# A perceiver block's fp8 layer: where the loop over tiles begins, on four engines

## The chip, the cores and the metric

The kernel runs on one core of a Trainium2 chip. The metric is device time in microseconds (us) for one launch; lower is better. The time before is the median of three runs, 4422.85 us (4418.86 to 4425.76).

## The reference, cut to what matters

The program is a chain of eleven layers on a residual stream of 1024 rows of 256 numbers. The change touches one of them, the cross attention of the fourth block, whose projections work on values rounded to fp8:

```python
def _L3_xattn_ref(hidden_states, cond, ...):
    ln_out = _ln(hidden_states, ln_w, ln_b)
    q = _ln(_fp8_linear_pertensor(ln_out, wq, wq_scale, q_in_scale).reshape(b, s, g, hpg, d), qln_w, qln_b)
    k = _ln(_fp8_linear_pertensor(ln_out, wk, wk_scale, k_in_scale).reshape(b, s, g, d), kln_w, kln_b)
    v = _fp8_linear_pertensor(ln_out, wv, wv_scale, v_in_scale).reshape(b, s, g, d)
    core = _gqa(q, k, v).reshape(b, s, nh * d)
    qx = _ln(_fp8_linear_pertensor(ln_out, wqx, wqx_scale, qx_in_scale).reshape(b, s, g, hpg, d), qxln_w, qxln_b)
    kx, vx = jnp.split(jnp.einsum('bsi,oi->bso', cond, w_kv_x), 2, axis=-1)
    kx = _ln(kx.reshape(b, sc, g, d), kxln_w, kxln_b)
    xout = _gqa(qx, kx, vx.reshape(b, sc, g, d)).reshape(b, s, nh * d)
    catq = _div_clamp_fp8(jnp.concatenate([core, xout], axis=-1), proj_smooth)
    return jnp.einsum('bsi,oi->bso', catq, wproj) * (proj_in_scale * proj_w_scale)
x = x + _L3_xattn_ref(_layernorm(x, axis=-1), ctx_2048, ...)
```

There are 16 query heads and 8 key heads of width 128, 64 own rows per sequence and 128 context rows.

## The kernel before

The layer (`l3_xattn`, from L3365) works through the stream in 8 tiles of 128 rows, two sequences each. Each engine has its own program, a loop over tiles 0 to 6 and a copy of the body for tile 7 behind it; a short stretch ahead of the loop does what the first tile needs. The order inside each program is written out by hand, and the engines meet at semaphores only. All the work of a tile is cut into phases, and phases of tile t+1 are mixed into tile t.

The phases and their names:

- **A head phase** (`HeadPhase`, L683) projects eight heads and normalises each. `fill` (PE, 4 matmuls of 512 columns into two banks, 8 in the trace, where an f32 matmul has two records), `stats_of` (DVE, 8 BN_STATS and 6 small instructions), `invert` (POOL), `normalise` (ACT, writes the rows), `turn` (PE, 8 transposes back into the same banks), `take` (ACT, copies them out and sets `ready`). Both `turn` halves wait for the rows, and whoever fills the pair of banks next first waits for `ready` (`free`, L3427). `x0` and `x1` are the context queries ("x" rows in the trace), `kc0` and `kc1` the context keys, `sk`, `sq0`, `sq1` the own keys and queries of the next tile. `vc0`, `vc1`, `sv` are values without a norm. x0, kc0, vc0, sk and sq1 share one pair of banks; x1, kc1, vc1, sq0 and sv the other.
- **Attention** (`WideAttention`, L784): `score` (PE), `shift` (DVE, subtracts the row maximum), `exponential` (ACT), `weigh` (DVE), `turn` (PE, 8 transposes), `take_turned` (ACT), `mix` (PE), `take_out` (DVE). `own` is the self attention, `cross` the one on the context, in two groups.
- **The norms of the next tile** (`Norm`, L188): `norm` and `ln` on DVE and POOL give `ln_y` (L213), `ln.tensor` (PE, L241, two transposes) and `ln.scalar` (ACT, L255) turn it, `round_inputs` (DVE, L3631) rounds it to fp8 as `xq`, from which every fill but those of the context reads.
- **The output projection** in four quarters (`part_of_y`, L3430: y0 to y3, 8 matmuls of 256 columns, 16 in the trace): y0 and y1 read the self attention, y2 and y3 the cross attention, each once `round_heads` (DVE) has rounded its half. `add_out` (DVE, L3651) adds the bank to the stream, once after y1 and once after y3. The norms of the next tile do not depend on this tile's sum; the stream tile they read is the next one.

In the loop body before, PE's order is: x0.fill, own.score, x1.fill, x0.turn, ln.tensor(t+1), kc0.fill, own.turn 0, x1.turn, own.mix 0, kc1.fill, own.turn 1, kc0.turn, own.mix 1, vc0.fill, kc1.turn, y0, vc1.fill, cross.score 0, sk.fill(t+1), cross.score 1, y1, sq0.fill, cross.turn 0 and on to sq1.turn, y2, y3. DVE's body begins with x0.stats_of, the first half of norm(t+1), own.shift, the second half, own.weigh, ln_y; it ends with round_heads, round_heads, add_out.

```python
                free(sq1, t)
                x0.fill(pe, t)
                pe.wait_ge(cross.out_taken.sem, cross.out_taken.value(t, 0))
                own.score(pe, t, 0)

                free(sv, t)
                x1.fill(pe, t)
                x0.turn(pe, t)
```

Of the kernel before, what the change touches and what calls it, by code (L numbers as in the profile page):

```python
# [82 lines left out]
def whole(program):  # L83

    for _ in program:
        pass
# [3278 lines left out]
def l3_xattn(nc, env):  # L3365
# [3 lines left out]
    with Layer(nc, env, "l3x") as L:  # L3369
# [15 lines left out]
        y_bank, ln_bank = t_bank[0][:, 0:D], t_bank[1]  # L3385
# [40 lines left out]
        def _(pe):  # L3426
# [4 lines left out]
            def part_of_y(t, n):  # L3431
                pe.wait_ge(cat_ready.sem, cat_ready.value(t, n + 1))
                return project(nc, y_bank, lambda c: cat[:, 8 * (n % 2) + c, :], lambda c: wproj[:, 8 * n + c, :], 8, start=n % 2 == 0, stop=n % 2 == 1)
# [14 lines left out]
            def tile(t, more):  # L3448
# [4 lines left out]

                free(sv, t)
                x1.fill(pe, t)
                x0.turn(pe, t)
                if more:
                    whole(ln.tensor(pe, t + 1, ln_bank))

# [3 lines left out]
                if more:  # L3463
                    pe.wait_ge(ln.ready.sem, ln.ready.value(t + 1))
                pe.wait_ge(tile_done.sem, tile_done.value(t, 0))
                own.turn(pe, t, 0)
                x1.turn(pe, t)
                own.mix(pe, t, 0)

                free(x1, t)  # L3470
                kc1.fill(pe, t)
                own.turn(pe, t, 1)
                kc0.turn(pe, t)
                own.mix(pe, t, 1)

                free(kc0, t)
                vc0.fill(pe, t)
                kc1.turn(pe, t)
                part_of_y(t, 0)
# [4 lines left out]
                cross.score(pe, t, 0)  # L3484

# [28 lines left out]
                part_of_y(t, 2)  # L3514
                part_of_y(t, 3).then_inc(y_ps.sem, 1)
# [5 lines left out]
        def _(act):  # L3521
# [7 lines left out]
            def tile(t, more):  # L3529
                o = Order(act, L.order["act"], t)  # L3530
                own.exponential(o, 0)

                x0.normalise(o)
                x0.take(o)
# [4 lines left out]

                x1.normalise(o)  # L3540
                own.take_turned(o, 0)
                x1.take(o)
# [40 lines left out]
        def _(pool):  # L3583
# [5 lines left out]
            def tile(t, more):  # L3589
                o = Order(pool, L.order["pool"], t)  # L3590
                x0.invert(o)
                if more:
                    o.t = t + 1
                    whole(norm.pool(o))
                    whole(ln.pool(o))
                    o.t = t
                x1.invert(o)
# [14 lines left out]
        def _(dve):  # L3612
# [45 lines left out]
            for phase in (sk, sq0, sq1):  # L3658
                phase.stats_of(first)
            def tile(t, more):  # L3660
                o = Order(dve, L.order["dve"], t)
                x0.stats_of(o)
# [5 lines left out]
                own.shift(o, 0)  # L3668
# [11 lines left out]
                x1.stats_of(o)  # L3680
# [4 lines left out]

                kc0.stats_of(o)
                own.take_out(o, 0)

                kc1.stats_of(o)
# [30 lines left out]
                round_heads(o, 1)  # L3720
                dve.wait_ge(y_ps.sem, y_ps.value(t))
# [819 lines left out]
```

## Time and profile before

| | us |
|---|---|
| median of 3 runs | 4422.85 |
| lowest, highest | 4418.86, 4425.76 |
| the profiled execution, its own time | 4422.6 |
| its span | 4420.8 |
| PE busy in the span | 3591.5 (81%) |
| DVE busy | 2633.6 (60%) |
| ACT busy | 1722.9 (39%) |
| POOL busy | 361.6 (8%) |
| mean granted TensorE clock | 0.792 |

The span is the stretch from the first to the last instruction of one profiled execution; 1.8 us lie around it. The shares are means over eleven layers. The layer in question runs from about 2920 us to 3742 us. The granted clock is 1.00 where TensorE has 2.4 GHz and 0.50 where it has 1.2 GHz.

### The profile page before, as it was taken

To read this page: it belongs to the slowest core of one execution; us is meant where nothing else is said; L and a number is where in the kernel's file an instruction comes from. 1 tells how busy PE (TensorE), PEld (TensorE's weight loads), DVE (VectorE), ACT (ScalarE), POOL (GpSimd) and SP (SyncE) were. 2 spreads that over 40 slices of the span, in tenths; PEclk is the share of its full clock that TensorE was granted. 3 is DMA by queue.
4 is the path that set the end of the run, shared out by engine and by line. 5 is a ranking of instruction groups with operands and counts; after the bars stand their busy time and mean duration, and the time that the engine had idled before them with its cause. 6 is when DMAs were issued, how large, how long until landed. Compare 5 with 4: busy or idle time off the path is not lost. (4 is left out here: it accounts for less than half of the span.)

```text
span 4420.8 us, 69997 instructions
## 1 busy us (share of the span) xinstructions
PE 3591.5 (81%) x26672; PEld 2566.4 (58%) x26672; DVE 2633.6 (60%) x5418; ACT 1722.9 (39%) x3305; POOL 361.6 (8%) x566
## 2 busy tenths in 40 slices
PE   7999998997787887753888776878888886878778
PEld 4655557876764555531555643535555555757667
DVE  6888885443367777876444363247667665453552
ACT  4888883111344343421333212224444442223323
POOL 3000000000000000000111000111111111121000
PEclk8555558998886666756988788989999997989787
DMA  2000001000010000010000014000000001200000
GB/s 78 1 0 0 0 0 72 0 0 19 7 36 20 0 0 0 0 58 2 5 5 5 5 59 134 0 3 3 3 5 3 3 3 35 82 0 0 1 1 10
DMA packets 44826, 72.66 MB, mean 16 GB/s; under 512 B 25805, under 2 KB 33489, under 8 KB 41045
## 3 DMA queue, kind: packets, MB, share of 16 engines
q1 hardware_dynamic: 36440, 70.54, 4.6%
q10 hardware_dynamic: 8256, 0.52, 0.2%
q8 instruction: 65, 1.06, 0.1%
q14 instruction: 65, 0.53, 0.0%
HBM read 67.91 MB, written 3.15 MB: 16 GB/s over the span
## 5 line engine op out<-in xcount | busy, mean ns | idle before, releaser
L1316 DVE TENSOR_SCALAR_CACHE_REDUCE l0x_ex<-l0x_s_ps 128x1024 f32<-128x1024 f32 x258 | 305.6, 1222 | 63.4 <-PE l0x_s_ps L1019 62.4
L1151 ACT ACTIVATE l0x_ex<-l0x_ex,l0x_neg_max,l0x_q_scale 128x2048 f32<-128x2048 f32 x128 | 267.9, 2093 | 52.4 <-DVE l0x_neg_max L1322 50.7
L1031 PEld LDWEIGHTS l0x_t_ps<-l0x_identb,l0x_pb 128*128 128x128 bf16 x2048 | 200.0, 142 | 109.4 <-issue 56.8
L1019 PE MATMUL l0x_s_ps<-l0x_kT,l0x_qT 64*128 64x512 bf16 x516 | 235.5, 600 | 32.9 <-ACT l0x_qT L1146 19.5
L1158 ACT ACTIVATE l0x_pt<-l0x_t_ps 128x1024 bf16<-128x1024 bf16 x256 | 246.3, 1014 | 32.2 <-PE l0x_t_ps L1031 32.2
L1031 PE MATMUL l0x_t_ps<-l0x_identb,l0x_pb 128*128 128x128 bf16 x2048 | 233.7, 304 | 6.8 <-ACT l0x_pt L1158 4.1
L1331 DVE TENSOR_SCALAR l0x_pb<-l0x_ex 128x2048 bf16<-128x2048 f32 x128 | 156.4, 1222 | 0.0
L263 PE MATMUL l3x_bank<-l3x_wproj,l3x_cat 128*128 128x256 f32 x512 | 120.7, 390 | 32.1 <-DVE l3x_cat L3345 32.1
L263 PE MATMUL l3x_bank<-l3x_w_kv_x,l3x_ctxT 128*128 128x512 f32 x256 | 129.8, 655 | 0.9 <-ACT l3x_ctx_q L762 0.9
L263 PEld LDWEIGHTS l3x_bank<-l3x_wproj,l3x_cat 128*128 128x128 f32 x512 | 96.1, 193 | 52.4 <-DVE l3x_cat L3345 38.7
L1019 PEld LDWEIGHTS l0x_s_ps<-l0x_kT,l0x_qT 64*128 64x128 bf16 x516 | 50.0, 121 | 129.4 <-issue 80.4
L840 ACT ACTIVATE l3x_e<-l3x_e 128x1024 f32<-128x1024 f32 x24 | 25.4, 1057 | 251.0 <-DVE l3x_e L860 251.0
L885 DVE TENSOR_TENSOR l2x_oT<-l2x_bank,l2x_bv 128x512 f32<-128x512 f32 x32 | 20.6, 686 | 168.6 <-PE l2x_bank L834 168.6
L834 PE MATMUL l2x_bank<-l2x_pt,l2x_v 128*128 128x64 f32 x512 | 95.9, 374 | 29.9 <-ACT l2x_pt L845 29.9
L707 PE MATMUL l3x_bank<-ident,l3x_rows 128*128 128x128 f32 x448 | 69.3, 294 | 61.1 <-ACT l3x_rows L755 61.1
L834 PEld LDWEIGHTS l2x_bank<-l2x_pt,l2x_v 128*128 128x128 f32 x512 | 93.1, 285 | 38.2 <-issue 32.0
L2112 PEld LDWEIGHTS l1a_bank<-l1a_u,l1a_gm 64*64 64x64 f32 x2048 | 109.4, 218 | 8.8 <-issue 7.9
L2112 PE MATMUL l1a_bank<-l1a_u,l1a_gm 64*64 64x8 f32 x2048 | 112.4, 249 | 0.0
L2252 ACT ACTIVATE l1a_decay<-l1a_bank 128x512 f32<-128x512 f32 x64 | 34.7, 594 | 190.9 <-PE l1a_bank L2093 190.9
L2093 PE MATMUL l1a_bank<-l1a_steps,l1a_after 128*128 128x512 f32 x132 | 105.3, 891 | 0.0
L707 PEld LDWEIGHTS l3x_bank<-ident,l3x_rows 128*128 128x128 f32 x448 | 53.4, 149 | 85.9 <-ACT l3x_rows L755 78.5
L2092 PE MATMUL l1a_bank<-l1a_same,l1a_later 64*128 64x512 bf16 x66 | 32.7, 495 | 82.4 <-DVE l1a_steps L2358 82.4
(740 smaller groups left out, 8651.6 us busy)
## 6 DMA issues: line engine op xcount, KB each, us to landing
l3x_wproj<-in_L_xattn_wproj SPq DMA_DIRECT2D x1, 4096.0 KB, 22.5
l3a_w<-in_L_attn_W SPq DMA_DIRECT2D x4, 1024.0 KB, 11.4
l2f_w<-in_L_ffn_w SPq DMA_DIRECT2D x1, 2816.0 KB, 12.4
l0x_ctxT<-in_ctxT SPq DMA_DIRECT2D x8, 256.0 KB, 3.0
l0a_wq<-in_L_attn_W_Q SPq DMA_DIRECT2D x1, 2048.0 KB
l0a_wk<-in_L_attn_W_K SPq DMA_DIRECT2D x1, 2048.0 KB
l0a_wv<-in_L_attn_W_V SPq DMA_DIRECT2D x1, 2048.0 KB, 8.0
l0a_wo<-in_L_attn_W_O SPq DMA_DIRECT2D x1, 2048.0 KB, 13.0
```

The lines of the kernel that those rows point to most:

```text
L263: ins = nc.tensor.matmul(out, wT(c), rhs(c), start=start and n == 0, stop=stop and n == chunks - 1)
L707: ins = self.L.nc.tensor.transpose(self.banks[u][:, h * P:(h + 1) * P], self.rows[:, 4 * u + h, :], self.L.env.ident[:])
L834: ins = self.L.nc.tensor.matmul(out[:, b * S:(b + 1) * S], self.v(half * 8 + h, b), self.pt[:, h, b * S:(b + 1) * S], start=True, stop=True)
L1019: ins = mm(s_ps[:, j * 512:(j + 1) * 512], qT[rows, h // 2, :], kT[rows, h // 2, j * 512:(j + 1) * 512], start=True, stop=True)
L1031: ins = nc.tensor.transpose(t_ps[:, j * P:(j + 1) * P], pb[:, h % 2, j * P:(j + 1) * P], identb[:])
L1151: s.activation(ex[:, h % 4, :], ex[:, h % 4, :], ACT.Exp, scale=q_scale[:, h:h + 1], bias=nb[:, h:h + 1], accum_out=sums[:, h:h + 1]).then ...
L1158: s.activation(pt[:, h % 2, c], t_ps[:, c], ACT.Copy).then_inc(o.up(pT_taken), 1)
L1316: v.tensor_scalar(ex[:, h % 4, c], s_ps[:, c], 1.0, None, ALU.mult, ALU.max, accum_out=mx[:, h, half:half + 1]).then_inc(o.up(scores_taken ...
L1331: v.tensor_scalar(pb[:, h % 2, :], ex[:, h % 4, :], MAGIC, -MAGIC, ALU.add, ALU.add).then_inc(o.up(probs), 1)
L2093: ins = mm(bank[4 + j][:], after[:], flat(steps_[:, 8 * j:8 * j + 8, :]), start=False, stop=True)
L2112: ins = mm(bank[6][r, h * HP:(h + 1) * HP], gm[r, h, :], u[r, h * HP:(h + 1) * HP], start=True, stop=True)
L2252: s.activation(flat(decay[:, h:h + 8, :]), bank[4 + j][:], ACT.Exp).then_inc(o.up(exp_ready if j else None), 1)
```

## The change

PE: x0.fill, own.score, x1.fill become a function `begin`, called once ahead of the loop for tile 0, and in the body for tile t+1 between y2 and y3. The body begins with x0.turn. ln.tensor(t+1) goes behind kc0.fill, x1.turn ahead of own.turn 0, kc1.fill ahead of own.mix 0, vc0.fill ahead of own.mix 1, vc1.fill directly behind kc1.turn, and y0 behind cross.score 0. ACT: the body begins with the rows of x0, the exponential comes behind x0.take, the rows of x1 ahead of ln.scalar. POOL: x1.invert goes between the two norms. DVE: x0.stats_of and own.shift of tile t+1 go to the end of tile t, ahead of the second add_out; the body begins with the first norm's statistics, then x1.stats_of; kc0.stats_of goes ahead of round_inputs, kc1.stats_of ahead of own.take_out 0.

```diff
@@ -3445,43 +3445,45 @@
             free(sq0, 0)
             sv.fill(pe, 0)
             sq1.turn(pe, 0)
-            def tile(t, more):
+
+            def begin(t):
                 free(sq1, t)
                 x0.fill(pe, t)
                 pe.wait_ge(cross.out_taken.sem, cross.out_taken.value(t, 0))
                 own.score(pe, t, 0)
-
                 free(sv, t)
                 x1.fill(pe, t)
+
+            begin(0)
+            def tile(t, more):
                 x0.turn(pe, t)
-                if more:
-                    whole(ln.tensor(pe, t + 1, ln_bank))
-
                 free(x0, t)
                 pe.wait_ge(ctx_loaded.sem, ctx_loaded.value(t))
                 kc0.fill(pe, t)
                 if more:
+                    whole(ln.tensor(pe, t + 1, ln_bank))
+                x1.turn(pe, t)
+                if more:
                     pe.wait_ge(ln.ready.sem, ln.ready.value(t + 1))
                 pe.wait_ge(tile_done.sem, tile_done.value(t, 0))
                 own.turn(pe, t, 0)
-                x1.turn(pe, t)
-                own.mix(pe, t, 0)
 
                 free(x1, t)
                 kc1.fill(pe, t)
+                own.mix(pe, t, 0)
                 own.turn(pe, t, 1)
                 kc0.turn(pe, t)
-                own.mix(pe, t, 1)
 
                 free(kc0, t)
                 vc0.fill(pe, t)
+                own.mix(pe, t, 1)
                 kc1.turn(pe, t)
-                part_of_y(t, 0)
 
                 free(kc1, t)
                 vc1.fill(pe, t)
                 pe.wait_ge(own.out_taken.sem, own.out_taken.value(t))
                 cross.score(pe, t, 0)
+                part_of_y(t, 0)
 
                 free(vc0, t)
                 if more:
@@ -3512,6 +3514,8 @@
                     sv.fill(pe, t + 1)
                     sq1.turn(pe, t + 1)
                 part_of_y(t, 2)
+                if more:
+                    begin(t + 1)
                 part_of_y(t, 3).then_inc(y_ps.sem, 1)
             with pe.Fori(0, TILES - 1) as t:
                 tile(t, True)
@@ -3528,18 +3532,17 @@
             sv.take(first)
             def tile(t, more):
                 o = Order(act, L.order["act"], t)
-                own.exponential(o, 0)
-
                 x0.normalise(o)
                 x0.take(o)
+                own.exponential(o, 0)
+
+                x1.normalise(o)
                 if more:
                     o.t = t + 1
                     whole(ln.scalar(o, ln_bank, scale=ln_w, bias=ln_b))
                     o.t = t
-
-                x1.normalise(o)
+                x1.take(o)
                 own.take_turned(o, 0)
-                x1.take(o)
 
                 kc0.normalise(o)
                 own.take_turned(o, 1)
@@ -3592,9 +3595,12 @@
                 if more:
                     o.t = t + 1
                     whole(norm.pool(o))
+                    o.t = t
+                x1.invert(o)
+                if more:
+                    o.t = t + 1
                     whole(ln.pool(o))
                     o.t = t
-                x1.invert(o)
                 kc0.invert(o)
                 kc1.invert(o)
                 if more:
@@ -3657,15 +3663,16 @@
             round_inputs(first)
             for phase in (sk, sq0, sq1):
                 phase.stats_of(first)
+            x0.stats_of(first)
+            own.shift(first, 0)
             def tile(t, more):
                 o = Order(dve, L.order["dve"], t)
-                x0.stats_of(o)
                 if more:
                     o.t = t + 1
                     first_norm, second_norm = norm.vector(o, tile_of(env.x, t + 1)), ln.vector(o, norm.y[:])
                     next(first_norm)
                     o.t = t
-                own.shift(o, 0)
+                x1.stats_of(o)
                 if more:
                     o.t = t + 1
                     whole(first_norm)
@@ -3677,16 +3684,13 @@
                     whole(second_norm)
                     o.t = t
 
-                x1.stats_of(o)
+                kc0.stats_of(o)
                 if more:
                     o.t = t + 1
                     round_inputs(o)
                     o.t = t
-
-                kc0.stats_of(o)
+                kc1.stats_of(o)
                 own.take_out(o, 0)
-
-                kc1.stats_of(o)
                 own.take_out(o, 1)
                 dve.wait_ge(own.out_taken.sem, own.out_taken.value(t, 1))
                 round_heads(o, 0)
@@ -3718,6 +3722,11 @@
                 round_heads(o, 0)
                 dve.wait_ge(cross.out_taken.sem, cross.out_taken.value(t, 2))
                 round_heads(o, 1)
+                if more:
+                    o.t = t + 1
+                    x0.stats_of(o)
+                    own.shift(o, 0)
+                    o.t = t
                 dve.wait_ge(y_ps.sem, y_ps.value(t))
                 add_out(o, tile_done)
                 dve.wait_ge(o.sem, o.at())
```

No instruction is added or taken away per tile. The two places below are those on which the steps of the next section rest. PE around the branch that closes the loop (COMPARE_AND_BRANCH); wqx is the weight of x0 and x1, own_k the own score, rows a turn, w_kv_x a context fill, pb the turn of the own probabilities, wproj a quarter of y. Before:

```order
L263 MATMUL l3x_bank<-l3x_wproj,l3x_cat 128x256 x8
L3432 REGISTER_ALU
L263 MATMUL l3x_bank<-l3x_wproj,l3x_cat 128x256 x8
L3516 REGISTER_ALU
L3516 COMPARE_AND_BRANCH
```

Now:

```order
L263 MATMUL l3x_bank<-l3x_wproj,l3x_cat 128x256 x8
L263 MATMUL l3x_bank<-l3x_wqx,l3x_xq 128x512 x4
L814 MATMUL l3x_bank<-l3x_own_k,l3x_own_q 64x64 x32
L263 MATMUL l3x_bank<-l3x_wqx,l3x_xq 128x512 x4
L3432 REGISTER_ALU
L263 MATMUL l3x_bank<-l3x_wproj,l3x_cat 128x256 x8
L3520 REGISTER_ALU
L3520 COMPARE_AND_BRANCH
```

The two fills and the score of the next tile went from behind the branch to between y2 and y3. DVE where its loop starts (the ISA row is the loop's own register work), now; ahead of it now stand, once, the 14 instructions of x0.stats_of and the 4 of own.shift that the body before began with:

```order
L860 TENSOR_TENSOR l3x_e<-l3x_bank,l3x_self_mx 128x512
L858 TENSOR_REDUCE l3x_self_mx<-l3x_bank 128x8
L860 TENSOR_TENSOR l3x_e<-l3x_bank,l3x_self_mx 128x512
L3734 UNCONDITIONAL_BRANCH
L3734 ISA
L206 BN_STATS l3x_n_stats<-x_stream 128x6
L207 ISA
L209 BN_AGGR l3x_n_mv<-l3x_n_stats 128x2
L210 REGISTER_ALU
L713 ISA
L715 BN_STATS l3x_x_stats<-l3x_bank 128x6 x4
```

The loop's first instruction is now the statistics of the stream, and it lies 18 instructions further on in DVE's program.

## Rows read from the trace of the kernel before

**Rows 1.** DVE's timeline (start, length, engine, line, what, [idle before]): `add_out`.

```profile
3061.61 0.48 DVE L3651 SCALAR_TENSOR_TENSOR x_stream<-l3x_bank,l3x_out_scale,x_stream 128x256 f32 x1 [3.89 <-PE l3x_bank L263]
...
3645.10 0.48 DVE L3651 SCALAR_TENSOR_TENSOR x_stream<-l3x_bank,l3x_out_scale,x_stream 128x256 f32 x1 [3.89 <-PE l3x_bank L263]
```

**Rows 2.** PE's timeline over one turn of the loop, 3150 to 3256 us.

```profile
3150.16 2.21 PE L263 MATMUL l3x_bank<-l3x_wproj,l3x_cat 128*128 128x256 f32 x9 [1.33 <-DVE l3x_cat L3345]
...
3161.84 2.08 PE L814 MATMUL l3x_bank<-l3x_own_k,l3x_own_q 128*64 128x64 f32 x64
...
3173.25 1.12 PE L707 MATMUL l3x_bank<-ident,l3x_rows 128*128 128x128 f32 x4 [5.70 <-ACT l3x_rows L755]
...
3176.42 0.69 PE L241 MATMUL l3x_bank<-ident,l3x_ln_y 128*128 128x128 f32 x2 [0.66 <-DVE l3x_ln_y L213]
3176.90 4.94 PE L263 MATMUL l3x_bank<-l3x_w_kv_x,l3x_ctxT 128*128 128x512 f32 x8
...
3212.44 3.70 PE L263 MATMUL l3x_bank<-l3x_wk,l3x_xq 128*128 128x512 f32 x8
...
3252.25 3.72 PE L263 MATMUL l3x_bank<-l3x_wproj,l3x_cat 128*128 128x256 f32 x16 [0.88 <-DVE l3x_cat L3345]
```

**Rows 3.** DVE's timeline behind the branch back, the same turn.

```profile
3158.59 0.48 DVE L3651 SCALAR_TENSOR_TENSOR x_stream<-l3x_bank,l3x_out_scale,x_stream 128x256 f32 x1 [3.89 <-PE l3x_bank L263]
3162.50 0.30 DVE L715 BATCH_NORM_STATS2 l3x_x_stats<-l3x_bank 128x6 f32<-128x128 f32 x1 [3.42 <-PE l3x_bank L263]
3164.74 1.48 DVE L715 BATCH_NORM_STATS2 l3x_x_stats<-l3x_bank 128x6 f32<-128x128 f32 x7 [1.95 <-issue]
...
3167.97 0.69 DVE L858 TENSOR_REDUCE l3x_self_mx<-l3x_bank 128x8 f32<-128x512 f32 x1
...
3170.63 0.40 DVE L213 TENSOR_SCALAR l3x_n_y<-x_stream,l3x_n_mv,l3x_n_rstd 128x256 f32 x1
...
3175.95 0.41 DVE L213 TENSOR_SCALAR l3x_ln_y<-l3x_n_y,l3x_ln_mv,l3x_ln_rstd 128x256 f32<-128x256 f32 x1
```

**Rows 4.** DMA queues (packets, MB, share): instruction queue in 3159.4:3161.5 and 3161.5:3164.

```profile
q14 instruction: 1, 0.01, 0.9%
...
q14 instruction: 1, 0.01, 1.2%
```

**Rows 5.** DVE's timeline where the loop is left for the last tile.

```profile
3646.73 0.89 DVE L715 BATCH_NORM_STATS2 l3x_x_stats<-l3x_bank 128x6 f32<-128x128 f32 x4 [1.15 <-PE l3x_bank L263]
```

**Rows 6.** POOL's and ACT's timeline: x0's scale, then its rows.

```profile
3169.34 0.20 POOL L746 TENSOR_TENSOR l3x_x_nmean<-l3x_x_mean,l3x_x_rstd 128x8 f32<-128x8 f32 x1
...
3171.71 2.89 ACT L755 ACTIVATE l3x_rows<-l3x_bank,l3x_x_nmean,l3x_x_rstd 128x128 f32<-128x128 f32 x8
```

**Rows 7.** PE's and ACT's timeline: own.turn 1, kc0.turn, kc0.take; kc1.turn, kc1.take.

```profile
3193.50 1.04 PE L821 MATMUL l3x_bank<-ident,l3x_pb 128*128 128x128 f32 x8
...
3195.55 1.45 ACT L762 ACTIVATE l3x_ctx_k<-l3x_bank,l3x_kxln_b,l3x_kxln_w 128x512 f32<-128x512 f32 x2
...
3201.04 1.04 PE L707 MATMUL l3x_bank<-ident,l3x_rows 128*128 128x128 f32 x8
...
3201.68 1.45 ACT L762 ACTIVATE l3x_ctx_k<-l3x_bank,l3x_kxln_b,l3x_kxln_w 128x512 f32<-128x512 f32 x2 [1.16 <-PE l3x_bank L707]
```

**Rows 8.** Windows (length, busy PE, PEld, DVE, ACT, POOL, granted clock, DMA); PE's timeline.

```profile
3172.40:3179.50 7.10, 5.32 (x14) 2.97 (x15) 6.79 (x22) 4.45 (x11) 0.63 (x2) 0.53 0.00 0
...
2951.82 6.62 PE L263 MATMUL l3x_bank<-l3x_wq,l3x_xq 128*128 128x512 f32 x8 [0.87 <-ACT l3x_own_k L762]
```

**Rows 9.** First tile: `ln_y` on DVE and the next tile's sk.fill on PE.

```profile
2981.56 0.41 DVE L213 TENSOR_SCALAR l3x_ln_y<-l3x_n_y,l3x_ln_mv,l3x_ln_rstd 128x256 f32<-128x256 f32 x1
...
3017.96 3.70 PE L263 MATMUL l3x_bank<-l3x_wk,l3x_xq 128*128 128x512 f32 x8
```

**Rows 10.** Last tile, PE: y2 of the tile before, and cross.score 1.

```profile
3636.66 3.72 PE L263 MATMUL l3x_bank<-l3x_wproj,l3x_cat 128*128 128x256 f32 x16 [1.33 <-DVE l3x_cat L3345]
...
3694.67 3.40 PE L814 MATMUL l3x_bank<-l3x_ctx_k,l3x_ctx_q 128*64 128x128 f32 x32 [3.00 <-DVE l3x_e L860]
```

## The prediction

> **What bounds the kernel now.** I read the timelines of PE and DVE over one turn of the loop of the fp8 layer. One turn is one `add_out` to the next: six turns take 3645.10 - 3061.61 = 583.5 us, 97.25 each [rows 1]. PE is the engine the others follow: between two y2 it works almost without a break, save one place. x1.fill ends at 3167.55, and x0.turn starts 5.70 us later, when ACT has written the first rows of x0 [rows 2]. The reader is to see why the rows are late: x0.fill was over by 3161.9, since own.score starts at 3161.84 [rows 2], but DVE, which takes the statistics, ended `add_out` at 3159.07, did one BN_STATS at 3162.50 and the other seven only from 3164.74 [rows 3]. The 3.43 us up to the first are the branch back, since where the loop is left without one, the first statistics come 1.15 us after `add_out` [rows 5]. The 1.95 us after the first wait for nothing ("issue"), and the instruction queue fetches a block in each of the two gaps [rows 4]. So 5.4 us of DVE's restart lie on the path x0.fill, rows, x0.turn, and behind it the layer norm of the next tile, whose ln.tensor waits again.
>
> **What the change does to that path.** I count from the start of y2 to the start of the next sk.fill; behind it nothing changes order up to the next y2. Before, that is 3212.44 - 3150.16 = 62.3 us [rows 2], in a turn of 97.5 us (`add_out` at 3158.59 [rows 3], y3's end 0.1 before the next one at 3252.25 + 3.72 [rows 2]); the mean turn is 0.25 shorter, so I take 62.0. Now, with y2 at 0:
>
> 1. y2 3.6, x0.fill 3.5, own.score 2.0, x1.fill 3.6, y3 3.7 (a fill as sk.fill 3.70 less the overlap of 0.15 with what follows, the rest as [rows 2] has it) without a wait: y3's rounding came 0.88 us too late behind y2, now 9 us of work cover it. y3 ends at 16.4.
> 2. x0.turn does not wait. x0.fill ends at 7.1, statistics 2.2 us after it at 9.3, scale at 11.4, the eight rows take 2.9 us [rows 6]: ready at 14.3, 1.9 us before PE asks. DVE's own.shift fits between. The stall of 5.70 us is gone.
> 3. kc0.fill needs x0.take, which needs x0.turn, and ln.tensor no longer stands between. From the start of kc1.turn to the end of kc1.take are 2.1 us, 1.1 beyond the turn [rows 7]. So kc0.fill runs from 18.4 to 22.0.
> 4. **What is late next is ln_y.** The second `add_out` now follows y3 at 16.4 instead of 7.3 + 0.9, ends at 16.95 (0.12 + 0.48), and only behind it DVE branches. Then 3.43 for the branch, 3.4 for x1.stats_of and the stream's statistics (3164.74 to 3167.97, and 0.2 for the one instruction ahead of the gap), 5.3 from n_y to the end of own.weigh, 0.4 for ln_y [rows 3]: 29.5. PE waits for it from 22.0: **7.6 us, the one large stall that is left.** Behind ln.tensor are queued x1.turn, own.turn, kc1.fill and all the rest of the tile.
> 5. The gap of 1.95 I take as gone. It lies directly behind the loop's first instruction, where a fetch happens; the loop's head now lies 18 instructions further on. Behind the second fetch DVE runs on to the end of ln_y, 11 us and some 40 instructions, without such a gap [rows 3], so edges lie much further apart than 18 instructions, and one that is met after some microseconds of work costs nothing. Lowest price of the gap in the changed kernel: none; highest: the full 1.95.
> 6. From 29.6: ln.tensor 0.5; x1.turn and own.turn at the low clock 2.2 and 2.1 (x0.turn's halves took 1.12 each, against 1.04 for a whole turn at the high one [rows 2, 7]); kc1.fill 4.9 as kc0.fill had it behind today's stall [rows 2]; own.mix 0 1.9: 41.1. own.turn 1, kc0.turn and kc0.take 3.6 [rows 7], of which 1.65 are a new wait, since own.mix no longer covers the take; vc0.fill 3.4; own.mix 1 1.9; kc1.turn and its take 2.15, with 1.1 of wait, also new; vc1.fill 3.5; cross.score 1.9; y0 3.6: sk.fill at 61.2. y0's own wait goes, because the rounding ends 2 us before it.
>
> So 62.0 becomes 61.2: the stall of 5.70, the gap of 1.95, the waits around x1.turn and the low clock over own.mix 0 go, and a wait of 7.6 and three of 1.1 to 1.65 come. **0.8 us a turn, 5 us for six.**
>
> The first and last tile are extra. At the first, DVE walks into the loop without a branch back: ln_y starts at 2981.56 plus 2.6 for x1.stats_of (as step 4 counts it, 3.4 less 0.8 for the stream) plus 0.4 because the exponential now stands behind x0.take, 2984.6 [rows 9]. From there the count of step 6 with turns and fill at the high clock, and about 1 us of small waits, is 29 us: sk.fill at 3014 instead of 3017.96, and up to 3016 if the clock falls, as it did under the fill at 2951.82. I take 3.3 us (2 to 4.3). At the last tile there is no norm and no branch. Before, y2 to cross.score 1 is 3694.67 - 3636.66 = 58.0 us [rows 10]. Now x1's rows are ready at 24.6 and the chain of step 6 without ln_y gives own.mix 1 at 38.7, then take_out 1.3, two roundings of 4.4 and own shift 2.7: cross.score 1 at 53.6. That is 4.4 less, and 1.4 more if the score then runs at the high clock. I take 4.8 (2.5 to 5.7).
>
> Sum: 5 + 3.3 + 4.8 = 13.1 us off the profiled execution's 4422.6, which stands 0.25 below the median: **4409.5 us**.
>
> **A rule against step 5.** The trace shows 1.95 us of DVE standing still with a fetch in it. The Trainium skill (Runtime: NRT & Kernel Launch, Instruction fetch mechanics) says that a taken branch out of the current two-page window forces a fetch before execution goes on, but of crossing a block's edge in sequence that it is "one DMA tail-bump, mostly hidden". By the first half the 3.43 us stay, which the trace bears out; by the second there would be no gap of 1.95 us to lose, and the sum would be that of the second rival below, 4421; here the trace speaks against it, since the gap stands behind the same instruction in every turn of this loop.
>
> **What is uncertain.** The clock after the new stall. The granted clock was 0.53 from 3172.4 to 3179.5, that is the lower level for nearly all of it, after PE had stood from 3167.55 [rows 8, 2]. Step 6 has own.mix 0 at the high clock, since no wait stands ahead of it any more. Lowest price: both turns and the fill at the high clock, 3.6 us less than taken, 22 us over six turns, if PE were back at once; the rows after the present stall speak against it, but a part of it can come. Highest: kc1.fill all at the low clock, 6.6 as at 2951.82 [rows 8], 1.7 us a turn more, 10 us over six. I take the value of the same stall today, since length and work behind it are nearest.
>
> **Rivals.**
> - *The forecast* (0.57): 4409.5, its own range 4402 to 4414.
> - *The clock comes back sooner* behind the stall (0.13): 1 to 3.6 us a turn less, 4388 to 4403.
> - *The gap of 1.95 us moves along with the loop's head*, because a restart always costs two fetches (0.12): ln_y 1.95 later in six turns, 11.7 us, 4421, no change. For it: it is in every turn. Against: it comes after one instruction, which looks like an edge.
> - *The clock stays low through kc1.fill* (0.12): 10 us more, 4419, no change.
> - *Slower*: the moved norm chain (0.06). ln_y now starts 8 us later relative to PE's work, and any further delay of it goes one to one into the turn, where today x0.turn and x1.turn absorb a part. Should DVE's restart meet two more gaps of 1.95, in x1.stats_of and in own.weigh, the turn grows by 3.9, six by 23.4: 4433. It decides from 3.7 us a turn upward (13.1 + 8.9 over six). For it: two gaps stand there today. Against: behind the second fetch none of today's instructions waits.
> - That x0.turn still waits has a margin of 1.9 us and would cost only what exceeds it.
>
> **Numbers.** About 0.2% (8.8 us) is what a measurement of this kernel can tell from no change: below 4414.0 is faster, above 4431.7 slower. The forecast is faster save its upper edge, the second case always, the third and fourth are in the same band, the fifth slower. Faster 0.67, same 0.27, slower 0.06. The range leaves out the ends of the sooner clock and the slower case: 4397 to 4421.
>
> **What would show it.** In the changed profile: x0.turn starts right behind y3; DVE's first statistics 3.4 us after `add_out`, and no idle "issue" of 1.95 behind it; PE waits 7 to 8 us for ln_y at L241, in front of it kc0.fill with a wait of about 1.1; waits of 1.6 and 1.1 at vc0.fill and vc1.fill on ACT; one stretch at the low clock per turn; a turn of 96.4 us. A wait at L241 of 9 us or more says that the gap is still there; kc1.fill above 6 us says that the clock is. I am wrong altogether if x0.turn still waits, or if a long wait stands at a fill or at cross.turn where I have none.

## The result, and the profile after

The changed kernel takes 4382.8 us (median of 4 runs, 4379.7 to 4386.3) against 4423.5 us for the kernel before (4 runs): a ratio of 0.9907, 95% interval 0.9891 to 0.9922. It is faster by 41 us. The forecast was 4409.5: the direction was right, the size was not, and the time lies outside the range of 4397 to 4421.

The span of the profiled execution fell from 4420.8 to 4377.9 us. Part of that is no effect: the layers ahead of this one took 8.4 us less, with the same instructions. So I measure the layer by itself, from VectorE's (DVE's) first statistics in it to its last `add_out`, in the timeline of DVE. Before:

```profile
2923.65 0.43 DVE L206 BATCH_NORM_STATS2 l3x_n_stats<-x_stream 128x6 f32<-128x256 f32 x1
...
3741.47 0.48 DVE L3651 SCALAR_TENSOR_TENSOR x_stream<-l3x_bank,l3x_out_scale,x_stream 128x256 f32<-128x256 f32 x1 [4.63 <-PE l3x_bank L263]
```

After:

```profile
2915.24 0.43 DVE L206 BATCH_NORM_STATS2 l3x_n_stats<-x_stream 128x6 f32<-128x256 f32 x1
...
3694.42 0.48 DVE L3657 SCALAR_TENSOR_TENSOR x_stream<-l3x_bank,l3x_out_scale,x_stream 128x256 f32<-128x256 f32 x1 [5.29 <-PE l3x_bank L263]
```

That is 817.8 us before and 779.2 after, 38.6 less. This measure repeats: another execution of the changed kernel gives 779.6, while its whole span is 10 us longer than the first; 9.1 us of that lie ahead of this layer. PE over one turn of the changed loop, to compare with [rows 2]:

```profile
3131.99 3.72 PE L263 MATMUL l3x_bank<-l3x_wproj,l3x_cat 128*128 128x256 f32 x16 [1.33 <-DVE l3x_cat L3345]
...
3144.63 3.62 PE L263 MATMUL l3x_bank<-l3x_wproj,l3x_cat 128*128 128x256 f32 x16
3148.08 1.04 PE L707 MATMUL l3x_bank<-ident,l3x_rows 128*128 128x128 f32 x8
3150.30 3.70 PE L263 MATMUL l3x_bank<-l3x_w_kv_x,l3x_ctxT 128*128 128x512 f32 x8 [1.18 <-ACT l3x_ctx_q L762]
3158.72 0.69 PE L241 MATMUL l3x_bank<-ident,l3x_ln_y 128*128 128x128 f32 x2 [4.72 <-DVE l3x_ln_y L213]
3159.20 1.91 PE L707 MATMUL l3x_bank<-ident,l3x_rows 128*128 128x128 f32 x8
3160.91 1.91 PE L821 MATMUL l3x_bank<-ident,l3x_pb 128*128 128x128 f32 x8
3162.61 4.26 PE L263 MATMUL l3x_bank<-l3x_w_kv_x,l3x_ctxT 128*128 128x512 f32 x8
3166.72 1.95 PE L831 MATMUL l3x_bank<-l3x_pt,l3x_own_v 128*128 128x128 f32 x16
3168.50 1.04 PE L821 MATMUL l3x_bank<-ident,l3x_pb 128*128 128x128 f32 x8
...
3172.05 3.70 PE L263 MATMUL l3x_bank<-l3x_w_kv_x,l3x_ctxT 128*128 128x512 f32 x8 [1.64 <-ACT l3x_ctx_k L762]
...
3179.51 3.70 PE L263 MATMUL l3x_bank<-l3x_w_kv_x,l3x_ctxT 128*128 128x512 f32 x8 [1.10 <-ACT l3x_ctx_k L762]
...
3188.59 3.60 PE L263 MATMUL l3x_bank<-l3x_wk,l3x_xq 128*128 128x512 f32 x8
```

The order is as forecast, with the small waits of 1.18, 1.64 and 1.10, x0.turn (3148.08) without a wait, and one large wait for `ln_y` at L241. But this wait is 4.72 us, not 7.6. DVE's timeline says why; compare [rows 3]:

```profile
3148.29 0.48 DVE L3657 SCALAR_TENSOR_TENSOR x_stream<-l3x_bank,l3x_out_scale,x_stream 128x256 f32 x1 [4.34 <-PE l3x_bank L263]
3149.44 0.43 DVE L206 BATCH_NORM_STATS2 l3x_n_stats<-x_stream 128x6 f32 x1 [0.67 <-DVEq L3733]
3150.02 0.18 DVE L209 BATCH_NORM_AGGREGATE l3x_n_mv<-l3x_n_stats 128x2 f32<-128x6 f32 x1 [0.15 <-DVEq L208]
...
3158.25 0.41 DVE L213 TENSOR_SCALAR l3x_ln_y<-l3x_n_y,l3x_ln_mv,l3x_ln_rstd 128x256 f32<-128x256 f32 x1
```

Between `add_out` and the first statistics there are 0.67 us, where 3.4 had been, and the gap of 1.95 is gone too. **The branch itself had become cheap.** The page's row of the queue that brings in DVE's instructions, before and then after:

```profile
q14 instruction: 65, 0.53, 0.0%
```

```profile
q14 instruction: 35, 0.29, 0.0%
```

30 packets fewer, which is five for each of six turns. In the turn from 3150 to 3247 us of the kernel before, this queue has 5 packets of 8192 B; in that from 3149 to 3240 us of the changed one it has none.

### The profile page after: what moved, and what is told of

Its sections match the earlier page's. It is cut to its first block and busy times, and to the rows that moved or that the text cites. A ratio compares the mean times of both kernels' runs of the same rounds, so it can differ in the third digit from the quotient of the medians.

```text
span 4377.9 us, 69990 instructions
## 1 busy us (share of the span) xinstructions
PE 3565.0 (81%) x26672; PEld 2558.8 (58%) x26672; DVE 2633.0 (60%) x5418; ACT 1723.9 (39%) x3305; POOL 359.3 (8%) x566
## 3 DMA queue, kind: packets, MB, share of 16 engines
q8 instruction: 65, 1.06, 0.1%
## 5 line engine op out<-in xcount | busy, mean ns | idle before, releaser
L1019 PE MATMUL l0x_s_ps<-l0x_kT,l0x_qT 64*128 64x512 bf16 x516 | 235.5, 600 | 32.8 <-ACT l0x_qT L1146 19.5
L834 PE MATMUL l2x_bank<-l2x_pt,l2x_v 128*128 128x64 f32 x512 | 91.8, 363 | 28.7 <-ACT l2x_pt L845 28.7
L885 DVE TENSOR_TENSOR l3x_cat<-l3x_bank,l3x_smooth_inv 128x512 f32<-128x512 f32 x64 | 41.2, 685 | 108.4 <-PE l3x_bank L834 68.7
L263 PEld LDWEIGHTS l3x_bank<-l3x_w_kv_x,l3x_ctxT 128*128 128x128 f32 x256 | 50.0, 206 | 87.9 <-issue 60.7
L263 PE MATMUL l2f_bank<-l2f_w,l2f_ln_yT 128*128 128x352 f32 x256 | 97.4, 512 | 0.0
```

Of the source, the lines that this page charges most:

```text
L263: ins = nc.tensor.matmul(out, wT(c), rhs(c), start=start and n == 0, stop=stop and n == chunks - 1)
L834: ins = self.L.nc.tensor.matmul(out[:, b * S:(b + 1) * S], self.v(half * 8 + h, b), self.pt[:, h, b * S:(b + 1) * S], start=True, stop=True)
L885: v.tensor_tensor(self.oT[:, h:h + 4, :], ps, by[:, h:h + 4].unsqueeze(2).broadcast_to([P, 4, P]), op).then_inc(o.up(self.out_taken if j e ...
L1019: ins = mm(s_ps[:, j * 512:(j + 1) * 512], qT[rows, h // 2, :], kT[rows, h // 2, j * 512:(j + 1) * 512], start=True, stop=True)
```

## What could be behind it

The queue brings DVE's program in by blocks. In what follows an edge is the border between two blocks, the head is the first instruction of the loop, the place is where the head lies in its block, and the restart is the time that DVE stands between `add_out` and its first operation behind the branch back.

**Theory A, the place in the blocks.** In the first tile of the kernel before, a packet arrives each time DVE has begun about 128 more instructions (5543, 5672 and 5804 of those recorded). So I take a block of 8192 B to hold 128 instructions, and the counts tell roughly where its edges lie: the old loop (269 instructions, the register and semaphore ones included) began 2 ahead of an edge and touched four blocks; the new one (268) begins 18 later, 16 behind that edge, and touches three. If DVE can hold four blocks and always brings in the next one, a loop over three stays, and a loop over four throws out its own beginning: five packets a turn. (DVE's turn has one semaphore instruction fewer in the trace after, 268 for 269, although the section on the change says that none is taken away.)

**Theory B, the order.** The instructions that now follow the branch, or the work that now overlaps it, hide the restart.

The experiments put idle instructions ahead of the loop (increments of a semaphore that nobody reads, 0.093 us each, where DVE waits 7.33 us for PE in the kernel before and 7.74 in the changed one). They move the loop in the blocks and change nothing in it. In the kernel before with three of them:

```diff
+            pad = L.sem("pad")
             first = Order(dve, L.sem("dve_first_order"))
@@
-            for phase in (sk, sq0, sq1):
+            for phase in (sk, sq0):
                 phase.stats_of(first)
+            for _ in range(3):
+                dve.sem_inc(pad, 1)
+            sq1.stats_of(first)
```

All results (ratio to the kernel before with its interval; the layer as measured above; a turn as a sixth of six; the packets of DVE's instruction queue in the whole program). The kernel before was timed again beside each set of runs: 4423.0 us beside the b runs and a110_old_place, 4419.5 beside a102_edge_ten_on, aln, v0_y3_in_the_middle and v1, 4423.4 beside the others. So two runs of different sets are compared by their ratios, or by the layer.

| run | edit | us | ratio | layer | turn | packets |
|---|---|---|---|---|---|---|
| before | | 4423 | | 817.8 | 97.2 | 65 |
| b1_one_extra | before + 1 | 4418.7 | 0.9997 (0.9983 to 1.0011) | 817.3 | 97.3 | 66 |
| b3_three_extra | before + 3 | 4401.4 | 0.9951 (0.9933 to 0.9968) | 800.1 | 94.0 | 35 |
| b20_twenty_extra | before + 20 | 4403.1 | 0.9955 (0.9937 to 0.9972) | 799.8 | 94.0 | 35 |
| after_again | | 4384.9 | 0.9908 (0.9893 to 0.9922) | 779.6 | 91.7 | 36 |
| a110_old_place | after + 110 | 4412.8 | 0.9987 (0.9976 to 0.9999) | 806.5 | 95.7 | 71 |
| a102_edge_ten_on | after + 102 | 4412.9 | 0.9981 (0.9972 to 0.9990) | 809.6 | 95.9 | 71 |
| a90_far_from_edge | after + 90 | 4387.8 | 0.9923 (0.9911 to 0.9936) | 779.4 | 91.8 | 41 |
| a90_twelve_inside | + 90, 12 inside | 4405.6 | 0.9966 (0.9953 to 0.9980) | 800.5 | 95.5 | 71 |
| aln_norm_turn_early | order, PE | 4414.5 | 0.9982 (0.9973 to 0.9991) | 809.9 | 95.7 | 35 |
| v0_y3_in_the_middle | order, PE | 4351.6 | 0.9847 (0.9831 to 0.9863) | 749.4 | 87.6 | 36 |
| v0_old_place | v0 + 110 | 4389.8 | 0.9927 (0.9914 to 0.9939) | 780.0 | 92.3 | 72 |
| v1_and_norms_first | order, three engines | 4376.6 | 0.9908 (0.9893 to 0.9924) | 772.3 | 90.9 | 35 |

## Experiments on the place

> The kernel before with ONE idle VectorE instruction (an increment of a semaphore that nobody reads) ahead of the l3x loop, in a stretch where VectorE waits over 7 us for TensorE. Theory A (place in the blocks: VectorE's code comes in blocks of 8192 B, 128 instructions; before, the loop of 269 instructions begins 2 ahead of a block's edge and touches four blocks, and the trace shows all of them and one more brought in again each turn; the changed kernel's loop begins 16 behind an edge, touches three, and the trace shows none brought in again): the head now lies 1 ahead of the edge, still four blocks: five fetches a turn, 2.9 to 3.1 us behind the branch, 4423 us within 0.2%. Theory B (the new order of the work, not the place, took the restart away): no change either, 4423 us. This kernel is the control for the next one.

> The kernel before with THREE such instructions ahead of the loop; nothing else differs from the kernel before. Theory A: the head lies 1 behind the edge, the loop touches three blocks: no fetch in the loop, the branch costs 0.3 us in place of 3.06, the gap of 1.95 is gone, the wait of x0.turn falls from 5.70 to about 1; a turn falls from 97.25 to 92.5 to 94.5, the time to 4388 to 4404 us. Theory B: 4423 us within 0.2%, five fetches a turn.

> The kernel before with TWENTY such instructions: the head lies 18 behind the edge, nearly as in the changed kernel (16). Theory A: as with three, within 0.15% of it (4388 to 4404 us). Theory B: 4423 us within 0.2%. What it lacks to the changed kernel's 4383 us is what the new order is worth at an equal place: by theory A at most 20 us, by theory B all 41.

One idle instruction changes nothing; **three make the kernel before 0.49% faster**, with not one instruction of the loop changed, and twenty do the same. Theory B is out as the whole cause. DVE and PE with three:

```profile
3159.12 0.48 DVE L3651 SCALAR_TENSOR_TENSOR x_stream<-l3x_bank,l3x_out_scale,x_stream 128x256 f32 x1 [3.89 <-PE l3x_bank L263]
3160.76 0.89 DVE L715 BATCH_NORM_STATS2 l3x_x_stats<-l3x_bank 128x6 f32<-128x128 f32 x4 [1.15 <-PE l3x_bank L263]
```

```profile
3170.38 0.66 PE L707 MATMUL l3x_bank<-ident,l3x_rows 128*128 128x128 f32 x4 [2.29 <-ACT l3x_rows L755]
```

The statistics come 1.15 us behind `add_out`, as where the loop is left in the kernel before [rows 5]. x0.turn waits 2.29 us where it had waited 5.70 [rows 2]; I had expected about 1. The turn falls by 3.3 us and not by the 4 to 5 that DVE gains, since its statistics now wait for x0.fill itself.

> The CHANGED kernel with 110 such instructions ahead of the loop (some 7 us of VectorE's time in a wait of 7.74 us for TensorE): its head lies 2 ahead of an edge, as in the kernel before. Theory A: four blocks, five fetches a turn, about 3 us behind the branch and 1.95 at the edge, the wait of ln.tensor for l3x_ln_y rises from 4.72 to 8 to 10, a turn from 92.1 to 95.5 to 97.5, the time to 4404 to 4420 us. Besides, the loop of the next layer (l3a, 311 instructions) then touches four blocks too, and its fetches must appear in every turn of it, which adds up to 20 us more. Theory B: 4383 us within 0.2%, no fetch in the loop.

The reverse, and it comes as theory A has it: 71 packets, and both gaps are back, at the new instructions:

```profile
3154.52 0.48 DVE L3657 SCALAR_TENSOR_TENSOR x_stream<-l3x_bank,l3x_out_scale,x_stream 128x256 f32 x1 [4.34 <-PE l3x_bank L263]
3158.39 0.43 DVE L206 BATCH_NORM_STATS2 l3x_n_stats<-x_stream 128x6 f32 x1 [3.39 <-issue]
3160.79 0.18 DVE L209 BATCH_NORM_AGGREGATE l3x_n_mv<-l3x_n_stats 128x2 f32<-128x6 f32 x1 [1.97 <-DVEq L208]
```

The wait at L241 is 9.25 us in place of 4.72. In the layer after this one (l3a), whose loop of 311 instructions now touches four blocks as well, the one branch back costs 3.04 us in place of 0.33. From this layer's last `add_out` to the span's end are 687.4 us, against 683.5 in the changed kernel; but in two other kernels with the same loss in l3a (a90_far_from_edge, v0_old_place) they are 683.4, so this part of the time is not settled by it. The 110 instructions took 10.5 us, not the 7 of the expectation, and the first tile up to sk.fill is 1.9 us longer (92.7 against 90.8).

> The CHANGED kernel with 102 idle VectorE instructions ahead of the loop, in place of the 110 of a110_old_place: its head lies 10 instructions ahead of a block's edge, not 2, so the loop still touches four blocks. Theory A (place in the blocks): five fetches a turn; the branch still costs about 3 us, and the second gap stands 8 instructions further on and is shorter by the time of these, some 1 us in place of 1.97, since the second block is asked for as soon as the first has landed. The wait of ln.tensor is 8.2 to 8.7 us in place of 9.25, a turn 94.5 to 95.5 us in place of 95.7, the time 4400 to 4412 us. Should the gap sit at l3x_n_mv again, it belongs to the operation and not to the edge. Theory B (the gap belongs to what was reordered): as the changed kernel, 4383 us.

```profile
3160.99 0.43 DVE L206 BATCH_NORM_STATS2 l3x_n_stats<-x_stream 128x6 f32 x1 [4.21 <-issue]
3161.57 0.18 DVE L209 BATCH_NORM_AGGREGATE l3x_n_mv<-l3x_n_stats 128x2 f32<-128x6 f32 x1 [0.15 <-DVEq L208]
3161.88 0.69 DVE L715 BATCH_NORM_STATS2 l3x_x_stats<-l3x_bank 128x6 f32<-128x128 f32 x3
3163.47 1.09 DVE L715 BATCH_NORM_STATS2 l3x_x_stats<-l3x_bank 128x6 f32<-128x128 f32 x5 [0.90 <-issue]
```

The second gap left l3x_n_mv and stands in the middle of a group of equal statistics, at 0.90 us: it belongs to the place in the code and to no operation. What I had not expected is that the first gap grew from 3.39 to 4.21, so that nothing was gained: the wait at L241 is 9.26 us, a turn 95.9, both above the expectation. In all six turns two packets start within 0.7 us of each other just behind the branch (here at 3158.00 and 3158.42); in a110_old_place only one starts there (3156.26), and the restart is 3.39. a90_twelve_inside below has such a pair too (3148.60 and 3149.09) and a restart of 4.17. So the pair goes with the longer restart; that the two packets delay each other was not tested by itself.

> The CHANGED kernel with 90 idle VectorE instructions ahead of the loop: its head lies 22 ahead of a block's edge, and its 268 instructions just fit into three blocks (106 + 268 = 374 of 384). Theory A1 (what counts is how many blocks the loop touches; four with the one brought in ahead are too many): no fetch in the loop, 0.3 us behind the branch, a turn of 92.1 us; 4383 us and up to 5 more, since the next layer's loop (l3a) now touches four blocks. Theory A2 (what counts is that the head lies ahead of an edge, a few instructions or some): fetches each turn, 4400 to 4412 us.

> As a90_far_from_edge, and twelve idle VectorE instructions INSIDE the loop as well, ahead of the wait for y_ps, where VectorE waits 4.34 us: they take 12 times 0.093 us, 1.1 us, of that wait. The loop now has 280 instructions and ends 2 behind the last edge: four blocks. Theory A1: five fetches a turn, 3.4 to 4.3 us between add_out and l3x_n_stats, but no second gap (the next edge is 22 instructions on); the wait of ln.tensor 7.3 to 8.3 us in place of 4.72, a turn 94 to 95.5 us, 4398 to 4408 us, which is the case that the prediction on record took the change for. Theory A2, or that only the head counts: within 0.1% of a90_far_from_edge.

```diff
+                for _ in range(12):
+                    dve.sem_inc(pad, 1)
                 dve.wait_ge(y_ps.sem, y_ps.value(t))
                 add_out(o, tile_done)
```

The two have the loop's head at the same place, 22 ahead of an edge, and differ only in where the loop ends. With 268 instructions it fits three blocks and the restart is free; with 280 it ends 2 instructions inside a fourth. It is the number of blocks that counts (A1), not the head's closeness to an edge. In the second kernel, as expected, there is one gap and no second:

```profile
3146.93 0.48 DVE L3657 SCALAR_TENSOR_TENSOR x_stream<-l3x_bank,l3x_out_scale,x_stream 128x256 f32 x1 [4.34 <-PE l3x_bank L263]
3151.58 0.43 DVE L206 BATCH_NORM_STATS2 l3x_n_stats<-x_stream 128x6 f32 x1 [4.17 <-issue]
3152.16 0.18 DVE L209 BATCH_NORM_AGGREGATE l3x_n_mv<-l3x_n_stats 128x2 f32<-128x6 f32 x1
```

Its restart is 4.17 - 0.67 = 3.5 us longer; six of them are 21.0, and the layer is 800.5 - 779.4 = 21.1 us longer. Whatever DVE loses at the branch goes one to one into the turn. PE's wait at L241, all six turns (groups by line, 3058 to 3610 us), in the changed kernel and then in this one:

```profile
L241 PE MATMUL l3x_bank<-ident,l3x_ln_y 128*128 128x128 f32 x12 | 3.9, 422 | 28.4 <-DVE l3x_ln_y L213 28.4
```

```profile
L241 PE MATMUL l3x_bank<-ident,l3x_ln_y 128*128 128x128 f32 x12 | 4.1, 449 | 50.1 <-DVE l3x_ln_y L213 50.1
```

What the four corners give, by the layer: old order 817.8 at the old place and 800.1 at a good one; new order 806.5 at the old place (a110_old_place) and 779.2 at its own. **Of the 38.6 us, 17.7 to 27.3 are the place and 11.3 to 20.9 the order**, by which is changed first. The 27.3 hold 1.9 us of the first tile, which is longer behind the 110 idle instructions; the six turns alone give 19.7 us for the place in the old order and 23.6 in the new. It is worth more in the new order; the likely reason is that there nothing absorbs a late `ln_y`.

## Experiments on the order

aln_norm_turn_early, v0_y3_in_the_middle and v1_and_norms_first stand at a good place (35 or 36 packets), so against the changed kernel only the order differs. v0_old_place has the order of v0_y3_in_the_middle and only the place differs.

> The CHANGED kernel with one part undone: ln.tensor stands ahead of kc0.fill on TensorE again, as in the kernel before. At the good place in the blocks. If the wait for l3x_ln_y is what bounds the middle of the turn, it is now 4.72 plus the 1.18 plus about 3.6 of kc0.fill, 9 to 9.6 us, with nothing put in it, kc0.fill comes 8 us later, and a turn grows by 3 to 4 us: 4403 to 4414 us. If kc0.fill's place is of no weight (VectorE bounds the stretch, not TensorE), it stays within 4379 to 4390 us.

```diff
                 x0.turn(pe, t)
+                if more:
+                    whole(ln.tensor(pe, t + 1, ln_bank))
                 free(x0, t)
...
                 kc0.fill(pe, t)
-                if more:
-                    whole(ln.tensor(pe, t + 1, ln_bank))
                 x1.turn(pe, t)
```

```profile
3179.91 0.69 PE L241 MATMUL l3x_bank<-ident,l3x_ln_y 128*128 128x128 f32 x2 [9.60 <-DVE l3x_ln_y L213]
```

The wait doubles to 9.60 and the turn grows by 3.9 us, about the length of kc0.fill: PE's order bounds the middle of the turn. The layer is then 9.8 us slower than the old order at a good place. So the new order without ln.tensor's move behind kc0.fill is a loss, and this one move turns it into a gain. The likely cost is y3 behind the fills, since `add_out`, the norms and `ln_y` all follow y3; the next run bears that out.

> The CHANGED kernel with the last quarter of the output projection (y3) between own.score and x1.fill, not behind x1.fill; nothing else. y3 then ends 3.6 us earlier, and VectorE adds it up right behind own.shift. Theory of the chain (y3's end, add_out, two norms, ln_y bounds ln.tensor): ln_y comes earlier, but by 1 to 2 us only, since x1.stats stands between the norms on VectorE and still waits for x1.fill; the wait of ln.tensor falls from 4.72 to about 3, the time to 4368 to 4378 us. Rival (VectorE's own work bounds the stretch): 4383 us within 0.2%.

```diff
                     begin(t + 1)
                 part_of_y(t, 3).then_inc(y_ps.sem, 1)
+                if more:
+                    begin_more(t + 1)
```

where `begin` is x0.fill and own.score, and `begin_more` is x1.fill. This beats both kernels: 4351.6 us, ratio 0.9847 to the kernel before. The changed kernel has 0.9907, so this is 27 us less by the ratios and 29.8 in the layer. I had expected 4368 to 4378. PE's middle of the turn:

```profile
3146.16 1.04 PE L707 MATMUL l3x_bank<-ident,l3x_rows 128*128 128x128 f32 x8
3148.37 3.70 PE L263 MATMUL l3x_bank<-l3x_w_kv_x,l3x_ctxT 128*128 128x512 f32 x8 [1.18 <-ACT l3x_ctx_q L762]
3153.95 0.44 PE L241 MATMUL l3x_bank<-ident,l3x_ln_y 128*128 128x128 f32 x2 [1.88 <-DVE l3x_ln_y L213]
3154.22 1.04 PE L707 MATMUL l3x_bank<-ident,l3x_rows 128*128 128x128 f32 x8
3155.47 1.06 PE L821 MATMUL l3x_bank<-ident,l3x_pb 128*128 128x128 f32 x8 [0.21 <-ACT l3x_ln_yT L255]
```

The wait at L241 falls from 4.72 to 1.88. The second part is the clock. Windows (length, busy PE, PEld, DVE, ACT, POOL, granted clock, DMA share, GB/s), the changed kernel and then this one:

```profile
3157.10:3164.00 6.90, 5.28 (x20) 4.56 (x21) 6.63 (x26) 4.71 (x10) 2.42 (x2) 0.51 0.00 0
```

```profile
3150.00:3160.00 10.00, 7.68 (x31) 4.07 (x30) 9.59 (x30) 6.69 (x16) 3.80 (x7) 1.00 0.00 0
```

In the changed kernel PE has 1.2 GHz from 3157.1 to 3164.0, around the wait's end, and x1.turn and own.turn take 1.91 each; here it has 2.4 GHz in the whole window, and they take 1.04 and 1.06. From ln.tensor's start to own.mix 0's end are 8.1 us in place of 9.8. My expectation had the first part and left out the second.

> The kernel v0_y3_in_the_middle (4351.6 us) with 110 idle VectorE instructions ahead of the loop, so that its head lies 2 ahead of an edge. Theory A: the restart of 4.5 us a turn is back and the wait of ln.tensor for l3x_ln_y rises from 1.88 to 6 to 6.5 us; the clock is low for part of what follows as in the changed kernel; a turn 91.5 to 93 us in place of 87.6, the time 4378 to 4392 us. If the chain had slack in this version, under 4370 us.

30.6 us longer in the layer (780.0 against 749.4), 35 us over all by the ratios: the place alone takes back the whole lead of this order over the changed kernel. The wait at L241 is 34.3 us over six turns, 5.7 each, a little under the 6 to 6.5 expected; x1.turn and own.turn take 1.91 each again.

> As v0_y3_in_the_middle, and VectorE makes both norms of the next tile, ln_y last, ahead of own.weigh, with x1.stats behind the second norm's statistics; GpSimd's order the same way. Theory of the chain: ln_y is there 5 to 6 us earlier than in the changed kernel, about when kc0.fill ends; the wait of ln.tensor falls from 4.72 to under 1 us, x1.turn waits about 1 us for its rows, own.turn comes 3 to 4.5 us earlier; a turn 88 to 89.5 us in place of 92.1, the time 4350 to 4366 us. Rival: own.turn then waits for own.weigh, which is now later, and half of it is given back: 4368 to 4380 us.

```diff
-                    next(first_norm)
-                    o.t = t
-                x1.stats_of(o)
-                if more:
-                    o.t = t + 1
                     whole(first_norm)
                     next(second_norm)
                     o.t = t
-                own.weigh(o, 0)
+                x1.stats_of(o)
                 if more:
                     o.t = t + 1
                     whole(second_norm)
                     o.t = t
+                own.weigh(o, 0)
```

GpSimd's order changes likewise. The time falls into the rival's band, but not by the rival's mechanism (that own.turn waits for own.weigh). ln.tensor no longer waits, as the theory had it; x1.turn behind it waits 3.66 us for its rows, where I had 1:

```profile
3148.70 0.38 PE L241 MATMUL l3x_bank<-ident,l3x_ln_y 128*128 128x128 f32 x2
3152.74 1.12 PE L707 MATMUL l3x_bank<-ident,l3x_rows 128*128 128x128 f32 x4 [3.66 <-ACT l3x_rows L755]
```

The rows wait for GpSimd (POOL), which scales x1's statistics:

```profile
3146.87 1.68 POOL L740 TENSOR_TENSOR l3x_x_rstd<-l3x_x_ve,neg_half 128x8 f32<-128x8 f32 x1 [2.03 <-DVE l3x_x_ve L734]
3148.62 1.27 POOL L743 TENSOR_TENSOR l3x_x_rstd<-l3x_x_rstd,l3x_scale_b 128x8 f32<-128x8 f32 x1
3149.97 1.18 POOL L746 TENSOR_TENSOR l3x_x_nmean<-l3x_x_mean,l3x_x_rstd 128x8 f32<-128x8 f32 x1
```

The last two take 0.20 us each in v0_y3_in_the_middle. Here they run while DVE does own.weigh's two products with both operands in SBUF (2.47 us from 3148.61 in this trace). The Trainium skill (SBUF — State Buffer, Who interferes with whom) says that such an operation contends with GpSimd's reads and that the later one waits; the rows agree, since each of the last two POOL operations ends within 0.1 us of the end of one of DVE's products, but no run here moves the two apart and nothing else.

## Why the prediction was wrong, step by step

By the layer's pieces, counted as the prediction counted them: the first tile up to sk.fill, the turns, and the last tile.

| piece | forecast | measured |
|---|---|---|
| first tile | -3.3 | -3.5 |
| six turns | -5 | -32.8 |
| last tile | -4.8 | -2.3 |
| layer | -13.1 | -38.6 |

1. **Steps 1 to 3 and the new waits of step 6 were right.** y3 without a wait, x0.turn at once, kc0.fill after 1.18 us (forecast 1.1), then 1.64 and 1.10 (forecast 1.65 and 1.1). From the end of own.mix 0 to sk.fill the forecast has 20.1 us, the rows 3188.59 - 3168.50 = 20.1.
2. **Step 4 failed: it kept the 3.43 us for the branch.** They measured 0.67. `ln_y` was forecast to end 29.5 us behind y2's start, and did at 3158.66 - 3131.99 = 26.7: 2.8 us a turn, 17 over six. This is the largest part of the miss. a90_twelve_inside gives the new order such a restart (4.17 us) and no second gap: its L241 wait is 50.1 / 6 = 8.4, which is the forecast's 7.6 and the 0.7 of the longer restart, and its turn is 95.5 us, where the forecast's 96.4 and 0.7, less the 1.7 of point 4, make 95.4.
3. **Step 5 was right in its result and wrong in its reason.** The gap of 1.95 went, not because the edge is now met after other work, but because no block is brought in at all. I had the two facts in hand, a block at each gap and an edge just behind the head, priced them one by one, and asked of the moved head only what it does to the edge, not whether the loop's blocks still have to be fetched. A count of the loop (269 instructions against blocks of 128) would have raised the question. The trace of the kernel before also held a row against step 4: in the next layer (l3a, 311 instructions), DVE stands only 0.71 us between the last operation ahead of the branch back and the first behind it, at 3922.17, and no packet arrives there.
4. **Step 6's clock was priced too high.** From ln.tensor to own.mix 0's end I had 11.5 us, measured 9.8: both turns take 1.7 from start to start at 1.2 GHz (forecast 2.2 and 2.1), and kc1.fill 4.1 instead of 4.9. That is 1.7 us a turn, 10 over six, and it does not come from step 4's error, since with the restart back (a90_twelve_inside) the same stretch takes 3170.70 - 3160.88 = 9.8 too.
5. **The last tile's sum had two slips.** From x1's rows at 24.6, step 6's own numbers give own.mix 1 at 44.6, not 38.7. From there take_out, two roundings of 4.4 each and the shift are 12.8 us, while the sum has 14.9. Measured are 45.2 for own.mix 1 and 58.4 for cross.score 1, not 53.6: 0.4 later than before. The 2.3 us that this tile did gain lie behind it.
6. **The rule against step 5.** Of the Trainium skill's two sentences (Runtime: NRT & Kernel Launch, Instruction fetch mechanics) the one on the branch carried the case: a target outside what is held is fetched first. I read it as a price on every branch back. The same section gives most engines' instruction memory as 32 KiB, 512 instructions, which is four of the blocks of 8192 B here and fits the runs: three blocks and one ahead stay, four and one ahead do not. It also says blocks of 16 KiB and a window of two; the packets here are of 8192 B, and with a window of two blocks of that size, 256 instructions, no loop of 268 could stay, as this one does. The crossing in sequence costs nothing in a90_twelve_inside, and 0.90 to 1.97 us where it lies within some instructions of a fetched head.

None of the four rivals was it. The rival "clock comes back sooner" had a band of 4388 to 4403, nearest of all, and about a third of the miss (10 of 27 us) is of its kind.

What stays open: why the layers ahead of this one differed by 8.4 us between two profiles with the same instructions (two profiles of the changed kernel differ there by 9.1, so the change need have no part in it), and why from this layer's last `add_out` to the span's end there were 679.3 us in the profile of the kernel before, 683.2 to 683.9 in ten others, and 686.6 to 687.4 in three.

## What to carry to other kernels

Count a hardware loop's instructions on each engine, register and semaphore ones included, and see from the instruction queue's packets whether it is brought in anew each turn; here a loop touches three blocks or four by where its head lies, for any length from 258 to 384 instructions. Where the head or the end of such a loop is near an edge, a few idle instructions ahead of it decide, and any edit that moves code can win or lose the restart without touching the loop. Before crediting an order with a gain, run the old order at the new place. And put the work that starts the longest chain over other engines (here y3, `add_out`, two norms) as early as its inputs allow, with what only fills an engine behind it.

## What the runs showed that I had not expected

- DVE's loop restart costs 0.67 us between the last and the first operation when its blocks stay, and 3.39 to 4.21 us when they do not; the second gap adds 1.97 us two instructions behind the head and 0.90 us ten behind it.
- One added instruction moved nothing and three moved 0.49% of an eleven-layer program.
- Loops further on shift too: with 90 to 110 idle instructions the branch back in l3a went from 0.33 to about 3 us.
